# Layer 3's first chunk in a four-layer mixture-of-experts kernel: the inputs scaled ahead are made one layer-2 unit later

## The chip, the core and the metric

The kernel runs on one core of a Trainium2 chip. The core has TensorE (PE, with PEld for its weight loads), VectorE (DVE), ScalarE (ACT), GpSimd (POOL) and SyncE (SP), which here only issues DMAs. The metric is the device time of one execution in microseconds (us), lower is better.

## The reference

Four blocks follow each other on x of shape 8 x 128 x 128 (batch, time, width), each of the form x = x + ffn(cond(x)). Cut to what matters here:

```python
# layer 2: cond is a low-rank and a dense product with a gelu, ffn is
for e in range(8):                                   # 8 experts, H=128, F=512
    hdn = gelu(flat @ w1[e] + b1[e])
    out = out + (hdn @ w2[e] + b2[e]) * comb[:, e:e+1]
# layer 3: cond is a recurrence over time
next_h = tanh(xw_t + prev_h @ Wh)
# ffn is a mixture over 12 experts, weighted on the input side
h = sum_e (x @ W1[e].T) * dw1[:, e]                  # = sum_e (x * dw1[:, e]) @ W1[e].T
h = gelu(h)
y = sum_e (h @ W2[e].T) * dw2[:, e] + dw3 @ b2
```

Layer 3 adds over the experts before its gelu, so the kernel multiplies the input by each expert's weight first and lets TensorE accumulate all 12 products in one PSUM bank.

## The kernel before

Time is cut into four chunks of 32 steps, which is 256 columns (32 steps x 8 batch rows) or two tiles of 128. The work of layers 0 to 2 is written out as a list UNITS of 176 units, and every engine runs its own loop over the same slots n = 0 to 177. A unit of stream B is half an expert of layer 2: two 128-column pieces of the up product on PE into bank U (each in three passes, since operands are split into a high and a low part), then a gelu with bias on ACT into `gated`, and two slots later half of the down product on PE into bank Y. When both halves of an expert are there, DVE adds Y times the expert's weight into `acc_b` (two instructions, one for each tile). The last 16 units, 160 to 175, are layer 2 of the last chunk. They are called B0 to B15 here, and "slot B10" is n = 170.

In these slots three other jobs run beside layer 2:

- layer 3's recurrence of chunk 0: two steps in each slot up to B11. A step is a small product on PE into ZR and a tanh on ACT into `h`. Every PE step waits for the tanh of the step before.
- layer 3's down weights: each slot DVE turns one of 12 (`l_dn_turned`), ACT copies it to its high part (`l_dn_hi`), and DVE makes the low part (`l_dn_lo`) of the first six.
- layer 3's first scaled inputs, which are what the change moves. For each pair of experts j = 0 to 5, DVE multiplies the input by the weights that a DMA spread over all partitions (`l_weighted<-l_bc,l_in`, called w0 to w5 here), ACT copies the product to its high part (`scaled_hi`, s0 to s5), and the low part (`scaled_lo`, low 0 to low 5) is made by POOL for j in POOL_FIRST = [0, 1, 2, 4] and by DVE for j = 3 and 5. `l_weighted` has two buffers, so w_j waits until low j-2 is made.

The table AHEAD holds one slot number for each j. DVE scales in slot AHEAD[j] + 1, ACT copies in slot AHEAD[j] + 2, and DVE makes its low parts in slot AHEAD[j] + 3. POOL has no slots: it takes its low parts in order, as they come.

Within a slot the engines keep this order, and each waits in order. ACT: first step's `h`, the unit's two gelus, `scaled_hi`, `l_dn_hi`, second step's `h`. PE: the up product, the first step's ZR, the down product of the unit two slots back, the second step's ZR. DVE: `acc_b` of the unit three slots back if it closes an expert, the turning, `l_dn_lo`, the low part, the scaling. After the loop DVE adds the last expert (B14 and B15) to `acc_b`, PE turns the sum into bank M (`layer_sum`) and goes on with layer 3's up products; DVE adds the residual in `layer_sums`.

Of the kernel before, what the change touches and what calls it, by code (L numbers as in the profile page):

```python
# [13 lines left out]
CT = 32  # L14
# [4 lines left out]
E3 = 12  # L19
# [25 lines left out]
def layer_units(stream, k, first=0, last=LU):  # L45

    return [(stream, i, k) for i in range(first, last)]


UNITS = L0_UNITS[:-HOLD] + layer_units("A", 0) + L0_UNITS[-HOLD:]  # L50
# [7 lines left out]
C3 = AT["A", 0, CHUNKS - 1]  # L58
# [8 lines left out]
def unit(n):  # L67

    return UNITS[n] if 0 <= n < len(UNITS) else ("", 0, 0)
# [30 lines left out]
L3_ADDR, L3_SCORE, L3_DW, W2_SLOT = [C3 + CT // 2 + i for i in (0, 1, 9, 6)]  # L100
POOL_FIRST = [0, 1, 2, 4]
W2_LATE = 6
AHEAD = [C3 + CT - 4 + j for j in range(E3 // 2)]


def x_early(n):
# [44 lines left out]
def at(start, n):  # L151

    return slice(start, start + n)
# [19 lines left out]
def adaln_ffn_program(nc, a, out):  # L173
    with ExitStack() as ctx:
# [413 lines left out]
        def _(sc):  # L588
# [106 lines left out]
            def scaled_first_high(j):  # L695
                sc.wait_ge(weighted_full, j + 1)
                sc.wait_ge(u_full, AT["B", 2 * j + 1, CHUNKS - 1] + 1)
                nc.scalar.activation(scaled[0][:, 2 * j:2 * j + 2, :].rearrange("p e n -> p (e n)"), l3_weighted[:, j % 2, :],
                                     ACT.Copy).then_inc(scaled_hi, 1)

            def l3_high(n):
                if n - 1 in AHEAD:
                    scaled_first_high(AHEAD.index(n - 1))
                if n in W1_SLOTS:
                    e = W1_SLOTS.index(n)
                    sc.wait_ge(w1_turned, e + 1)
                    nc.scalar.activation(l3_up[0][:, e, :], l3_up_turned[:, e, :], ACT.Copy).then_inc(w1_hi, 1)
                if 0 <= n - 1 - W2_SLOT < E3:
                    e = n - 1 - W2_SLOT
                    sc.wait_ge(w2_turned, e + 1)  # L710
                    nc.scalar.activation(l3_dn[0][:, e, :, :], l3_dn_turned[:, e, :, :], ACT.Copy).then_inc(w2_hi, 1)
# [48 lines left out]

            for n in range(SLOTS, AHEAD[-1] + 3):
                if n - 2 in AHEAD:
                    scaled_first_high(AHEAD.index(n - 2))

            def idle(*_):
                pass
# [34 lines left out]
        def _(dve):  # L801
# [3 lines left out]
            def tt(out, in0, in1, op):  # L805
                return v.tensor_tensor(out=out, in0=in0, in1=in1, op=op)  # L806
# [231 lines left out]
            def taken(*name):  # L1038
                dve.wait_ge(m_full, m_of(*name) + 1)
                return bank_of(*name)  # L1040
# [89 lines left out]
            def layer_sums(n):  # L1130

                stream, i, k = unit(n - 3)
                if (stream, i) == ("A", LU - 1):
                    x = x1[:, at(k * N, N)]
                    tt(x, x, taken("sum0", k)[:, 0:N], ALU.add).then_inc(m_free, 1)
                    tt(z1m[:, :].rearrange("p (t b) -> p t b", b=B), taken("zp", k)[:, N:].rearrange("p (t b) -> p t b", b=B),
                       rank_mask[:, 0:B].unsqueeze(1).to_broadcast([P, CT, B]), ALU.mult).then_inc(z_scaled, 1)
                if (stream, i) == ("B", LU - 1):
                    tt(x3[:, at(k * N, N)], x1[:, at(k * N, N)], taken("sum1", k)[:, 0:N], ALU.add).then_inc(m_free, 1)
                stream, i, k = unit(n - 4)  # L1140
                if (stream, i) == ("A", LU - 1):
                    dve.wait_ge(l2_gelu, k + 1)
                    own(v.tensor_copy(l2_x[0][:, :], l2_in[:, :]))
                    tt(l2_x[1][:, :], l2_in[:, :], l2_x[0][:, :], ALU.subtract).then_inc(m_free, 1)
# [72 lines left out]
            def l3_scale_first(j):  # L1217

                if j == 0:
                    dve.wait_ge(dw_loaded, 16)  # L1220
                if j >= 2:
                    dve.wait_ge(*low_of(j - 2))
                tt(l3_weighted[:, j % 2, :].rearrange("p (e n) -> p e n", e=2), bc_of(j),
                   l3_in.unsqueeze(1).to_broadcast([P, 2, N]), ALU.mult).then_inc(weighted_full, 1)

            def l3_low_first(j):

                dve.wait_ge(scaled_hi, j + 1)
                dve.wait_ge(y_full, DOWNS.index(AT["B", 2 * j + 1, CHUNKS - 1]) + 1)
                tt(scaled[1][:, 2 * j:2 * j + 2, :].rearrange("p e n -> p (e n)"), l3_weighted[:, j % 2, :],  # L1230
                   scaled[0][:, 2 * j:2 * j + 2, :].rearrange("p e n -> p (e n)"), ALU.subtract).then_inc(scaled_odd, 1)
# [16 lines left out]
            def l3_ahead(n):  # L1248

                if n - 3 in AHEAD and AHEAD.index(n - 3) not in POOL_FIRST:  # L1250
                    l3_low_first(AHEAD.index(n - 3))
                if n - 1 in AHEAD:
                    l3_scale_first(AHEAD.index(n - 1))
# [62 lines left out]

            add_layer(len(UNITS) - 1)

            layer_sums(len(UNITS) + 2)
            for n in range(SLOTS, AHEAD[-1] + 4):  # L1320
                l3_ahead(n)

            def l3(c, route_next):
                m0, y0 = M0_L3 + c * M_L3, Y0_L3 + c * Y_L3
# [44 lines left out]
        def _(pe):  # L1369
# [262 lines left out]
            def idle(*_):  # L1632
                pass
# [148 lines left out]
```

## Time and profile before

| what | us |
|---|---|
| median of 3 runs | 625.62 (625.25 to 625.73) |
| the profiled execution, whole | 626.07 |
| its span from first to last instruction | 624.3 |
| PE busy in it | 601.4 (96%) |
| mean granted TensorE clock | 0.995 of full speed |

The profiled execution lies 0.45 us over the median, and 1.8 us of its time lie outside the span. Times in the rows below are us from the start of the span.

### The profile page before, as it was taken

Reading aid. Unit: us, or ns where it says so; the run is one execution under the profiler, and the core shown is the slowest. Engines: PE = TensorE matmul, PEld = TensorE weight load, DVE = VectorE, ACT = ScalarE, POOL = GpSimd, SP = SyncE. Lnnn points to the kernel's source line nnn. Section 1 sums busy time; section 2 is a strip of 40 time slices with the busy share of each in tenths; the row PEclk is TensorE's granted clock in tenths of the full one; section 3 lists DMA queues with packets and bytes.
Section 4 is the critical chain, followed back from the end, with each engine's and each line's share of the span. In section 5 each row is a group of like instructions: output and inputs, shape, how many; then the busy total and the mean of one; then the engine's idle time right before and its main releaser. Section 6 shows DMA issues by size and latency. Waiting matters only on the chain.

```text
span 624.3 us, 12421 instructions
## 1 busy us (share of the span) xinstructions
PE 601.4 (96%) x4526; PEld 562.4 (90%) x4526; DVE 348.0 (56%) x1221; ACT 287.5 (46%) x955; POOL 110.7 (18%) x328
## 2 busy tenths in 40 slices
PE   8889999999999999999999999999899999999896
PEld 8678788889999999999999999999889889898895
DVE  4865655765464455455553563158858665775414
ACT  3275645645655456455564556646723323311110
POOL 3134121111111111111111110000201221321410
PEclk9999999999999999999999999999999999999999
DMA  8998000000000000000000000090202102002000
GB/s 253 383 270 135 1 1 2 2 2 1 2 2 1 2 1 2 2 2 1 2 1 1 2 2 2 17 187 21 83 2 69 40 5 102 6 5 104 8 1 8
DMA packets 47477, 26.98 MB, mean 43 GB/s; under 512 B 28424, under 2 KB 42680, under 8 KB 46904
## 3 DMA queue, kind: packets, MB, share of 16 engines
q1 hardware_dynamic: 45392, 25.71, 15.2%
q8 instruction: 36, 0.59, 0.4%
q10 hardware_dynamic: 2024, 0.48, 0.4%
q14 instruction: 25, 0.20, 0.1%
HBM read 25.61 MB, written 0.57 MB: 42 GB/s over the span
## 4 chain that ended last, share of the span: by engine, by line
PE 80%; DVE 11%; ACT 3%; issue 2%; DMA 2%; POOL 1%; SPq 0%; DVEq 0%; POOLq 0%
PE Y L1371 32%; PE U L1371 29%; PE HH L1371 8%; PE ZR L1371 7%; PE M L1371 5%; DVE acc_a L814 2%; DMA l_bc<-dw 1%; DVE acc_b L814 1%; DVE rh L814 1%; DVE rank L846 1%; POOL scaled_lo L566 1%; DVE relu L806 1%; ACT gated L648 0%; DVE cmp_a L806 0%; DVE l_dn_turned L1092 0%
## 5 line engine op out<-in xcount | busy, mean ns | idle before, releaser
L1371 PE MATMUL Y<-l_dn,gated 128*128 128x128 f32 x1152 | 162.8, 284 | 1.8 <-ACT gated L648 0.8
L1371 PEld LDWEIGHTS Y<-l_dn,gated 128*128 128x128 f32 x1152 | 141.1, 192 | 3.5 <-issue 1.7
L648 ACT ACTIVATE gated<-U,b1T 128x256 f32<-128x256 f32 x256 | 106.7, 473 | 0.0
L1371 PE MATMUL U<-l_x_hi,l_up_hi 128*128 128x256 f32 x256 | 82.7, 323 | 0.0
L630 ACT ACTIVATE h<-ZR,rnn_b 128x8 f32<-128x8 f32 x128 | 34.2, 267 | 90.0 <-PE ZR L1371 87.6
L814 DVE SCALAR_TENSOR_TENSOR fresh<-zr_s,cand 128x8 f32<-128x8 f32 x128 | 21.4, 167 | 94.9 <-ACT cand L626 92.4
L1371 PE MATMUL U<-l_x_hi,l_up_lo 128*128 128x256 f32 x256 | 72.0, 281 | 0.0
L1371 PE MATMUL U<-l_x_lo,l_up_hi 128*128 128x256 f32 x256 | 71.9, 281 | 0.0
L550 POOL TENSOR_SCALAR zh<-zr_s 128x8 f32<-128x8 f32 x128 | 25.7, 200 | 253.4 <-ACT zr_s L622 253.4
L626 ACT ACTIVATE cand<-HH 128x8 f32<-128x8 f32 x128 | 22.7, 178 | 97.0 <-PE HH L1371 97.0
L1371 PE MATMUL U<-scaled_hi,l_up_hi 128*128 128x256 f32 x192 | 58.0, 302 | 1.7 <-POOL scaled_lo L566 1.7
L1371 PE MATMUL U<-scaled_hi,l_up_lo 128*128 128x256 f32 x192 | 54.3, 283 | 0.0
L1371 PE MATMUL U<-scaled_lo,l_up_hi 128*128 128x256 f32 x192 | 54.2, 282 | 0.0
L1371 PEld LDWEIGHTS HH<-rh,gru_u 128*128 128x128 f32 x256 | 39.3, 190 | 13.6 <-DVE rh L814 12.5
L1371 PEld LDWEIGHTS U<-l_x_hi,l_up_hi 128*128 128x128 f32 x256 | 48.7, 190 | 0.5 <-issue 0.4
L1371 PEld LDWEIGHTS U<-l_x_hi,l_up_lo 128*128 128x128 f32 x256 | 48.7, 190 | 0.0
L1371 PEld LDWEIGHTS U<-l_x_lo,l_up_hi 128*128 128x128 f32 x256 | 48.3, 189 | 0.0
L1371 PE MATMUL ZR<-h_gru,gru_u 128*128 128x8 f32 x256 | 47.3, 257 | 0.0
L1371 PEld LDWEIGHTS ZR<-h,rnn_w 128*128 128x128 f32 x256 | 41.0, 190 | 6.7 <-ACT h L630 4.4
L814 DVE SCALAR_TENSOR_TENSOR acc_a<-Y,mix,acc_a 128x128 f32<-128x128 f32 x96 | 33.7, 351 | 22.7 <-PE Y L1371 19.9
L1371 PE MATMUL HH<-rh,gru_u 128*128 128x8 f32 x256 | 40.5, 230 | 5.2 <-DVE rh L814 4.4
L1371 PEld LDWEIGHTS HH<-h_gru,gru_u 128*128 128x128 f32 x256 | 39.8, 192 | 4.4 <-DVE h_gru L814 3.1
(263 smaller groups left out, 1202.8 us busy)
## 6 DMA issues: line engine op xcount, KB each, us to landing
l_bc<-dw SPq DMA_DIRECT2D x4, 1536.0 KB, 6.7
stage<-L_ffn_W_dram SPq DMA_DIRECT2D x4, 768.0 KB, 10.4
w_raw<-L_ffn_W_dram SPq DMA_DIRECT2D x12, 256.0 KB, 7.0
l_up_raw<-L_ffn_W_dram SPq DMA_DIRECT2D x1, 2048.0 KB, 9.7
l_up_raw<-L_ffn_w_dram SPq DMA_DIRECT2D x1, 2048.0 KB, 14.6
l0f_up<-L_ffn_w_dram SPq DMA_DIRECT2D x1, 768.0 KB, 7.0
l0f_dn<-L_ffn_w_dram SPq DMA_DIRECT2D x1, 768.0 KB, 8.8
x<-x_dram SPq DMA_DIRECT2D x1, 512.0 KB, 4.2
```

The costliest lines, as they stand in the source:

```text
L550: own(nc.gpsimd.tensor_scalar(zh[:, :], zr_s[:, 0, :], -0.5, 0.5, ALU.mult, ALU.add))
L566: nc.gpsimd.tensor_tensor(out=scaled[1][:, 2 * j:2 * j + 2, :].rearrange("p e n -> p (e n)"), in0=source[:, j % 2, :], in1=scaled[0][:, 2 ...
L626: nc.scalar.activation(cand[:, :], HH[:, at(N + step % CT * B, B)], ACT.Tanh).then_inc(gru_cand, 1)
L630: nc.scalar.activation(h3[:, at((step + 1) * B, B)], ZR[:, at(step % CT * B, B)], ACT.Tanh, bias=rnn_b[:, 0:1]).then_inc(rnn_h, 1)
L648: last = nc.scalar.activation(gated[:, n % 4, h * N:(h + 1) * N], U[n % 2][:, h * N:(h + 1) * N], ACT.Gelu, bias=b1T[:, col:col + 1])
L806: return v.tensor_tensor(out=out, in0=in0, in1=in1, op=op)
L814: return v.scalar_tensor_tensor(out=out, in0=in0, scalar=scalar, in1=in1, op0=op0, op1=op1)
L846: own(v.tensor_reduce(out=grp(rank, g, n), in_=ca, axis=AX.X, op=ALU.add))
L1371: return nc.tensor.matmul(out, lhsT, rhs, start=start, stop=stop, skip_group_check=shared)
```

## The change

The table AHEAD starts one slot later, so that w_j, s_j and DVE's low parts stand one slot on. Two pieces of DVE's code after the loop change places; the `for` loop there runs from 178 to AHEAD[-1] + 4, which is 177 before and 178 now, so that it has no turns in either kernel and the exchange moves nothing.

```diff
-AHEAD = [C3 + CT - 4 + j for j in range(E3 // 2)]
+AHEAD = [C3 + CT - 3 + j for j in range(E3 // 2)]
...
             add_layer(len(UNITS) - 1)
 
-            layer_sums(len(UNITS) + 2)
             for n in range(SLOTS, AHEAD[-1] + 4):
                 l3_ahead(n)
+            layer_sums(len(UNITS) + 2)
```

AHEAD was 168 to 173 and is 169 to 174. PE, POOL and SP have the same rows in the same order in both kernels.

ScalarE around slot B10, before. The first pair of gelus is unit B10's, the second B11's, and `l_dn_hi` is a copy of a down weight.

```order
L648 ACTIVATE gated<-U,b1T 128x256 x2
L698 ACTIVATE scaled_hi<-l_weighted 128x512
L711 ACTIVATE l_dn_hi<-l_dn_turned 128x512
L630 ACTIVATE h<-ZR,rnn_b 128x8 x2
L648 ACTIVATE gated<-U,b1T 128x256 x2
```

The same place on ScalarE now.

```order
L648 ACTIVATE gated<-U,b1T 128x256 x2
L711 ACTIVATE l_dn_hi<-l_dn_turned 128x512
L630 ACTIVATE h<-ZR,rnn_b 128x8 x2
L648 ACTIVATE gated<-U,b1T 128x256 x2
L698 ACTIVATE scaled_hi<-l_weighted 128x512
```

The copy s0 no longer stands between B10's gelus and the two recurrence steps, but behind B11's gelus. Each later copy moves in the same way, and s5 stands alone in slot B16, behind the last gelus.

VectorE in slots B9 and B10, before. The `acc_b` pair is the expert of units B6 and B7.

```order
L1092 STREAM_TRANSPOSE l_dn_turned<-w_raw 128x4x4x32
L806 TENSOR_TENSOR l_dn_lo<-l_dn_turned,l_dn_hi 128x512
L806 TENSOR_TENSOR l_weighted<-l_bc,l_in 128x512
L814 SCALAR_TENSOR_TENSOR acc_b<-Y,comb_l,acc_b 128x128 x2
L1092 STREAM_TRANSPOSE l_dn_turned<-w_raw 128x4x4x32
L806 TENSOR_TENSOR l_dn_lo<-l_dn_turned,l_dn_hi 128x512
```

The same place on VectorE now.

```order
L1092 STREAM_TRANSPOSE l_dn_turned<-w_raw 128x4x4x32
L806 TENSOR_TENSOR l_dn_lo<-l_dn_turned,l_dn_hi 128x512
L814 SCALAR_TENSOR_TENSOR acc_b<-Y,comb_l,acc_b 128x128 x2
L1092 STREAM_TRANSPOSE l_dn_turned<-w_raw 128x4x4x32
L806 TENSOR_TENSOR l_dn_lo<-l_dn_turned,l_dn_hi 128x512
L806 TENSOR_TENSOR l_weighted<-l_bc,l_in 128x512
```

The first scaling w0 stands behind one sum, one turning and one low part of a weight that it stood ahead of.

VectorE from slot B13 to the end of layer 2, before. The scalings are w4 and w5, the low parts 3 and 5, and the sums those of B10/B11, B12/B13 and B14/B15.

```order
L806 TENSOR_TENSOR l_weighted<-l_bc,l_in 128x512
L814 SCALAR_TENSOR_TENSOR acc_b<-Y,comb_l,acc_b 128x128 x2
L806 TENSOR_TENSOR scaled_lo<-l_weighted,scaled_hi 128x512
L806 TENSOR_TENSOR l_weighted<-l_bc,l_in 128x512
L814 SCALAR_TENSOR_TENSOR acc_b<-Y,comb_l,acc_b 128x128 x2
L806 TENSOR_TENSOR scaled_lo<-l_weighted,scaled_hi 128x512
L814 SCALAR_TENSOR_TENSOR acc_b<-Y,comb_l,acc_b 128x128 x2
L806 TENSOR_TENSOR x<-x,M 128x256
```

The same place on VectorE now.

```order
L814 SCALAR_TENSOR_TENSOR acc_b<-Y,comb_l,acc_b 128x128 x2
L806 TENSOR_TENSOR l_weighted<-l_bc,l_in 128x512
L806 TENSOR_TENSOR scaled_lo<-l_weighted,scaled_hi 128x512
L806 TENSOR_TENSOR l_weighted<-l_bc,l_in 128x512
L814 SCALAR_TENSOR_TENSOR acc_b<-Y,comb_l,acc_b 128x128 x2
L806 TENSOR_TENSOR scaled_lo<-l_weighted,scaled_hi 128x512
L814 SCALAR_TENSOR_TENSOR acc_b<-Y,comb_l,acc_b 128x128 x2
L806 TENSOR_TENSOR x<-x,M 128x256
```

Only w4 has changed places, with the sum of B10/B11; w5 and the low parts 3 and 5 keep theirs among VectorE's rows, and low 5 stood ahead of the last sum before as well.

## Rows read from the trace of the kernel before

**Rows 1.** The page: busy time of each engine over the span.

```profile
PE 601.4 (96%) x4526; PEld 562.4 (90%) x4526; DVE 348.0 (56%) x1221; ACT 287.5 (46%) x955; POOL 110.7 (18%) x328
```

**Rows 2.** Waits from 436 to 458: who waited, for whom, total, times, longest.

```profile
ACT scaled_hi L698 <- DVE l_weighted L806: 2.3, 3, 1.2
...
PE ZR L1371 <- ACT h L630: 1.7, 1, 1.7
```

**Rows 3.** The chain that ended last, from 435: start, duration, what.

```profile
435.30 7.62 DMA l_bc<-dw
```

**Rows 4.** TensorE's timeline: start, duration, line, operation, [idle before, releaser].

```profile
441.05 0.39 PE L1371 MATMUL ZR<-h,rnn_w 128*128 128x8 f32 x2
...
445.03 0.39 PE L1371 MATMUL ZR<-h,rnn_w 128*128 128x8 f32 x2 [1.66 <-ACT h L630]
...
454.23 2.05 PE L1371 MATMUL Y<-l_dn,gated 128*128 128x128 f32 x16 [0.78 <-ACT gated L648]
...
456.98 0.71 PE L1371 MATMUL M<-ident,acc_b 128*128 128x128 f32 x4 [0.27 <-DVE acc_b L814]
...
457.77 0.47 PE L1371 MATMUL U<-scaled_hi,l_up_hi 128*128 128x256 f32 x1
```

**Rows 5.** ScalarE's timeline, slots B9 to B15.

```profile
439.32 0.27 ACT L630 ACTIVATE h<-ZR,rnn_b 128x8 f32<-128x8 f32 x1 [0.48 <-PE ZR L1371]
...
441.47 0.27 ACT L630 ACTIVATE h<-ZR,rnn_b 128x8 f32<-128x8 f32 x1 [0.48 <-PE ZR L1371]
441.64 0.83 ACT L648 ACTIVATE gated<-U,b1T 128x256 f32<-128x256 f32 x2
443.67 0.63 ACT L698 ACTIVATE scaled_hi<-l_weighted 128x512 fp32r<-128x512 f32 x1 [1.20 <-DVE l_weighted L806]
444.21 0.61 ACT L711 ACTIVATE l_dn_hi<-l_dn_turned 128x512 fp32r<-128x512 f32 x1
...
445.62 0.83 ACT L648 ACTIVATE gated<-U,b1T 128x256 f32<-128x256 f32 x2
...
448.04 0.83 ACT L648 ACTIVATE gated<-U,b1T 128x256 f32<-128x256 f32 x2
448.75 0.64 ACT L698 ACTIVATE scaled_hi<-l_weighted 128x512 fp32r<-128x512 f32 x1
...
453.30 0.87 ACT L648 ACTIVATE gated<-U,b1T 128x256 f32<-128x256 f32 x2
```

**Rows 6.** VectorE's timeline, slots B9 to the last sum.

```profile
441.21 0.65 DVE L806 TENSOR_TENSOR l_dn_lo<-l_dn_turned,l_dn_hi 128x512 fp32r<-128x512 f32 x1
442.94 0.69 DVE L806 TENSOR_TENSOR l_weighted<-l_bc,l_in 128x512 f32<-128x512 f32 x1 [1.09 <-DMA l_bc<-dw]
443.55 0.60 DVE L814 SCALAR_TENSOR_TENSOR acc_b<-Y,comb_l,acc_b 128x128 f32<-128x128 f32 x2
444.19 0.71 DVE L1092 STREAM_TRANSPOSE l_dn_turned<-w_raw 128x512 f32<-128x512 f32 x1
444.82 1.37 DVE L806 TENSOR_TENSOR l_dn_lo<-l_dn_turned,l_dn_hi 128x512 fp32r<-128x512 f32 x1
...
447.35 0.64 DVE L806 TENSOR_TENSOR l_weighted<-l_bc,l_in 128x512 f32<-128x512 f32 x1
...
453.02 1.79 DVE L806 TENSOR_TENSOR l_weighted<-l_bc,l_in 128x512 f32<-128x512 f32 x1
...
455.57 0.69 DVE L806 TENSOR_TENSOR scaled_lo<-l_weighted,scaled_hi 128x512 fp32r<-128x512 f32 x1 [0.23 <-DVE acc_b L814]
456.31 0.61 DVE L814 SCALAR_TENSOR_TENSOR acc_b<-Y,comb_l,acc_b 128x128 f32<-128x128 f32 x2
```

**Rows 7.** GpSimd's timeline, its low parts 0, 1 and 4.

```profile
444.38 1.27 POOL L566 TENSOR_TENSOR scaled_lo<-l_weighted,scaled_hi 128x512 fp32r<-128x512 f32 x1 [74.11 <-ACT scaled_hi L698]
447.54 1.61 POOL L566 TENSOR_TENSOR scaled_lo<-l_weighted,scaled_hi 128x512 fp32r<-128x512 f32 x1 [1.89 <-ACT scaled_hi L698]
...
453.00 1.27 POOL L566 TENSOR_TENSOR scaled_lo<-l_weighted,scaled_hi 128x512 fp32r<-128x512 f32 x1 [1.99 <-ACT scaled_hi L698]
```

## The prediction, made blind

> **What bounds the kernel now.** I read the page first: TensorE is busy for 601.4 of 624.3 us [rows 1], so whatever does not reach TensorE's order of work is worth nothing, and the time to be won in a stretch is what TensorE idles there. Next come the waits of the stretch from 436 to 458, which holds every instruction that the change moves. Three entries matter. ScalarE waited three times, 2.3 us together, for `l_weighted`, and TensorE waited once, 1.7 us, for ScalarE's `h` [rows 2]. The timelines tie them together. The transfer of the spread weights `l_bc` takes 7.62 us and lands at 442.92 [rows 3], VectorE's first scaling w0 waits 1.09 us for it and starts at 442.94 [rows 6], and ScalarE's copy s0 stands idle 1.20 us for w0 and starts at 443.67 [rows 5]. Behind s0 in ScalarE's order are the copy of a down weight and the recurrence's tanh of slot B10. TensorE's next recurrence product needs that tanh, so it starts at 445.03 after 1.66 us of nothing [rows 4]. This is a stall of the whole chain, not of a side job.
>
> A second limit follows it. From B12 to B15 ScalarE has two gelus, a scaled copy and a weight copy in each slot and no idle time: its gelus start at 448.04 and 453.30 three slots apart, 1.753 us a slot [rows 5]. TensorE's last two down products wait for the last gelus and start at 454.23 [rows 4], their sums on VectorE start at 456.31 [rows 6], and the closing product with the sum starts 0.67 us behind that, at 456.98 [rows 4]. So I ask for two things: when the gelus of B15 now start, and whether VectorE is free when the last Y is full.
>
> **ScalarE and TensorE from slot B10.** With s0 gone from slot B10, ScalarE goes from the gelus to the weight copy and the tanh, as in the slots before it, where one `h` follows the same one of the last slot by 2.15 us (439.32 and 441.47) [rows 5]. TensorE's product stands 2.15 after 441.05, at 443.20, not at 445.03 [rows 4]: 1.83 us earlier. ScalarE's `h` of B11 is at 443.62, its gelus at 443.79, and s0 is wanted 0.71 later (448.04 to 448.75), at 444.50 [rows 5].
>
> Is w0 there by then? VectorE ends its low part of slot B9 at 441.86 and now goes straight into the sum of B6/B7, at about 441.78, since neighbours overlap by some 0.08. The steps of the rows are 0.64 for a sum, 0.63 for a turning and about 0.57 for a low part that nothing disturbs (the 0.65 of its own less that overlap) [rows 6]: turning at 442.42, low part at 443.05, w0 from 443.62 to 444.30. The transfer landed 0.70 before that, and s0 has 0.2 to spare. So the transfer's wait is covered by 1.8 us of work that VectorE had to do anyway.
>
> From s0 on ScalarE steps by 0.54 to the weight copy [rows 5], by 0.52 to the tanh and by 0.15 to the gelus of B12 (estimates, the first from the 0.54 and the 0.63 durations, the second from the 0.17 of 441.47 to 441.64): 445.71, where it was 448.04. Three slots of 1.753 lead to 450.97 for the gelus of B15: 2.33 us earlier. The 0.50 beyond 1.83 is the copy that slot B11 had to wait for (the second of the three waits). TensorE keeps up: before, too, it was TensorE that waited 0.78 for the last gelus [rows 4], so I cost nothing for it. Its last down products start at 451.90 and, 2.05 long, fill Y by 453.95.
>
> **VectorE and GpSimd in the same slots.** Here a stall can come back. The rows show that a VectorE operation of the form TENSOR_TENSOR and a GpSimd one do not run together. The low part at 444.82 took 1.37 where its twin took 0.65, and ended 0.54 after GpSimd's (444.38 + 1.27 = 445.65) [rows 6, 7]. In the other direction GpSimd's low 1 took 1.61 when it started at 447.54 in w2 (447.35 to 447.99): 1.27 from w2's end, less than 0.1 of it unexplained [rows 6, 7]. And w5 began at 453.02, 0.02 after low 4, and took 1.79 [rows 6, 7]. The first to start keeps the other out. Sums and turnings show no such loss (0.60 and 0.71 throughout).
>
> With that I go through VectorE's new order. Sum of B8/B9 and the turnings lie between the scalings. w1 at 444.85 to 445.50, ahead of low 0 (s0 ends 445.13, GpSimd follows 0.08 later, as 444.38 follows the 444.30 at which s0 ended before [rows 5, 7]), which then runs to 446.77. w2 waits for low 0 and runs 446.81 to 447.47; low 1 ends 448.74. w3 waits for low 1 and starts at 448.78, while low 2 may start when s2 is made, at 448.89: VectorE is first by 0.11. w3 ends 449.46 and low 2 450.73; the sum of B10/B11 fits between; w4 450.77 to 451.46; low 3 451.38 to 452.07; w5 452.11 to 452.80, ahead of low 4, which could start at 452.42 (s4 at 451.70): first by 0.31. Low 4 then holds GpSimd's side until 454.07. The sum of B12/B13 is not held. s5 is ScalarE's, from 452.84 to 453.47, so that low 5 could begin at 453.51, and it is kept out until 454.07 and ends 0.54 later, at 454.61.
>
> **The closing sum.** Low 5 stands ahead of the last `acc_b` on VectorE. Before, it ran at 455.57 to 456.26, just in front of the sum at 456.31, and cost nothing since Y was not full yet [rows 6]. Now Y is full at 453.95 and the sum could start at 453.99, but low 5 lets it start only at 454.53, a new wait of 0.54. Queued behind it are that sum, TensorE's closing product, and all of layer 3. The product starts 0.67 later, at 455.20.
>
> **Sum.** 456.98 - 455.20 = 1.78 us: 1.83 for the recurrence's stall, plus 0.50 on ScalarE, less 0.54 for low 5 in front of the sum (0.01 is rounding). Layer 3's first products follow from the same product, before 0.79 behind it (457.77) [rows 4]. They want the pair j = 5 only at the eleventh of twelve experts, and low 4 and low 5 are both made before the first, so nothing is late there. From there to the end the order and the data are those of before, and what waits, waits on TensorE. No DMA is issued by another time but those that follow the chain. I take the gain through to the end unchanged.
>
> The profiled execution took 626.07, so it would take 624.29. The median of the runs is 0.45 lower, 625.62, and I predict 625.62 - 1.78 = **623.8 us**.
>
> One rule of the Trainium skill speaks against this change: SBUF — State Buffer, section "Who interferes with whom", says that a VectorE instruction with two SBUF inputs and a GpSimd instruction that reads SBUF take the same read port, and that the second to issue waits for all of the first. By it low 5 pays and the sum is 1.78; the 1.37 and 1.79 of this trace agree with it. Were there no such exclusion, the same walk gives low 5 from 453.41 to 454.10, the closing product at 454.69, and a gain of 2.29.
>
> **Rivals.**
>
> *The low part is not in the way: 2.3 us, 623.3.* This holds if w5 and s5 come early enough, or the two engines overlap better than at 444.82, so that the closing sum starts when Y is full. For it speaks that low 5 needs to be only 0.54 earlier. Against it are the rows with 1.37 and 1.79. Chance 0.12.
>
> *GpSimd wins a race.* If it starts low 2 ahead of w3 (my margin is 0.11), w3 ends near 450.63, s3 and with it the gelus of B15 slip by 0.75, and low 5 ends near 455.0: the closing product at 455.60, a gain of 1.4, 624.2. If it is low 4 ahead of w5 (margin 0.31, and this is what happened before, by 0.02), low 5 ends near 455.6 and the gain is 0.8, 624.9. Chance 0.13 and 0.07.
>
> *No change: the wait only moves.* If w0 came late for s0 in slot B11, the tanh of the second step is late there as well. But B11 has the last recurrence step of the chunk, and no product waits for it until layer 3. Also both races lost together: low 4 and low 5 then end near 455.7 and 456.4, the closing product at 456.95, gain 0.03. Time 625.0 to 625.6. Chance 0.09.
>
> *Slower.* The mechanism is again low 5 ahead of the last sum, now later than it was: low 4 starts first, w5 waits for it, s5 for w5, low 5 for s5, four links of which each now comes a slot nearer to the end. It turns the gain into a loss when low 5 ends after 456.39 (0.08 overlap before 456.31), which is 1.78 after my 454.61; at 457.7 it would cost 1.3, time 626.9. That needs one more GpSimd instruction (1.27) in front of it than I can find, on top of both races. Chance 0.05.
>
> **How the numbers follow.** My forecast (gain 1.55 to 2.05) has 0.54; the five cases above 0.12, 0.13, 0.07, 0.09 and 0.05. The bounds are the walk without exclusion (2.3) and the late low 5 (0.8); 0.1 to 0.2 on each side covers that the medians of three runs scatter by 0.25. Range 623.1 to 624.9, which leaves 0.09, 0.05 and part of the 0.07 out. A measurement of this kernel tells about 0.2%, 1.25 us, from no change. Faster by that: 0.54 + 0.12 and most of the 0.13, 0.77. Within: 0.18. Slower: 0.05.
>
> **What would show it.** Right: no idle time of TensorE before a recurrence product near 443.2; ScalarE's s0 without a wait worth 0.1; gelus of B15 near 451.0; a VectorE low 5 of over 1 us or a late start of the closing sum behind it; the closing product near 455.2. Wrong: a wait of s0 or s3 for `l_weighted`, a w3 or w5 of over 1.2 us, or a span after the closing product that isn't the old 167.3 us (624.3 - 456.98). I would be wrong above all if a scaling and a GpSimd low part swapped places in that closest race.

## The result, and the profile after

Over 20 runs of each kernel the ratio of the changed kernel to the one before is 0.9964, 95% interval 0.995 to 0.9979. The medians are 624.34 us for the changed kernel and 626.30 us for the one before. Applied to the 625.62 us that the prediction started from, the ratio is 623.4 us, a gain of 2.25 us (1.3 to 3.1). Predicted were 623.8, a gain of 1.78, and a range of 623.1 to 624.9.

The profiled execution after took 624.21 us with a span of 622.5, where the one before took 626.07 with 624.3. That difference of 1.86 us is not the change alone. ScalarE's gelus of B8, before anything that the change moves, start at 436.12 and started at 437.33, so 1.21 us came from the early part of the execution. From those gelus to the closing product is 17.52 us and was 19.65 (437.33 to 456.98 [rows 4]): 2.13 us, the change's own. And from the closing product to the end of the span are 168.9 us, where they were 167.3: 1.5 us were lost again, for a reason given below. So all readings below use the distance from the gelus of B8. In the kernel before they are this row of ScalarE's timeline, two pairs of gelus ahead of B10's at 441.64 [rows 5]:

```profile
437.33 0.83 ACT L648 ACTIVATE gated<-U,b1T 128x256 f32<-128x256 f32 x2
```

One profiled execution in the experiments, that of the kernel with AHEAD one slot less than before, was a disturbed one with a span of 646.6 us, and only its waits are relied on, not its two distances in the table.

The timeline of ScalarE in the changed kernel, from the gelus of B8 on; `scaled_hi` is the copy of a scaled input.

```profile
436.12 0.83 ACT L648 ACTIVATE gated<-U,b1T 128x256 f32<-128x256 f32 x2
...
440.43 0.83 ACT L648 ACTIVATE gated<-U,b1T 128x256 f32<-128x256 f32 x2
...
442.58 0.83 ACT L648 ACTIVATE gated<-U,b1T 128x256 f32<-128x256 f32 x2
443.30 0.64 ACT L698 ACTIVATE scaled_hi<-l_weighted 128x512 fp32r<-128x512 f32 x1
...
444.49 0.85 ACT L648 ACTIVATE gated<-U,b1T 128x256 f32<-128x256 f32 x2
...
449.76 0.89 ACT L648 ACTIVATE gated<-U,b1T 128x256 f32<-128x256 f32 x2
```

Slot B10 (440.43) to slot B11 (442.58) is again the ordinary 2.15 us, where it was 3.98 [rows 5], and no row carries a wait for `l_weighted`. B11 to B12 is 1.91, where it was 2.42.

TensorE in the changed kernel: the product that stalled before [rows 4], the last down products, and the closing product.

```profile
441.99 0.39 PE L1371 MATMUL ZR<-h,rnn_w 128*128 128x8 f32 x2
...
450.70 2.05 PE L1371 MATMUL Y<-l_dn,gated 128*128 128x128 f32 x16 [0.68 <-ACT gated L648]
...
453.64 0.71 PE L1371 MATMUL M<-ident,acc_b 128*128 128x128 f32 x4 [0.46 <-DVE acc_b L814]
```

The 1.66 us of waiting for ScalarE's `h` are gone. The last down products start 14.58 us after B8's gelus (16.90 before), 2.32 earlier; the closing product 2.13 earlier.

VectorE in the changed kernel, w0 to w5 with the last two low parts and sums.

```profile
442.40 0.68 DVE L806 TENSOR_TENSOR l_weighted<-l_bc,l_in 128x512 f32<-128x512 f32 x1
...
443.62 0.65 DVE L806 TENSOR_TENSOR l_weighted<-l_bc,l_in 128x512 f32<-128x512 f32 x1
...
445.46 0.68 DVE L806 TENSOR_TENSOR l_weighted<-l_bc,l_in 128x512 f32<-128x512 f32 x1
...
447.32 0.69 DVE L806 TENSOR_TENSOR l_weighted<-l_bc,l_in 128x512 f32<-128x512 f32 x1 [0.56 <-POOL scaled_lo L566]
...
449.27 0.69 DVE L806 TENSOR_TENSOR l_weighted<-l_bc,l_in 128x512 f32<-128x512 f32 x1 [0.74 <-POOL scaled_lo L566]
449.88 0.68 DVE L806 TENSOR_TENSOR scaled_lo<-l_weighted,scaled_hi 128x512 fp32r<-128x512 f32 x1
450.60 0.69 DVE L806 TENSOR_TENSOR l_weighted<-l_bc,l_in 128x512 f32<-128x512 f32 x1
...
452.29 0.78 DVE L806 TENSOR_TENSOR scaled_lo<-l_weighted,scaled_hi 128x512 fp32r<-128x512 f32 x1 [0.48 <-DVE acc_b L814]
452.99 0.59 DVE L814 SCALAR_TENSOR_TENSOR acc_b<-Y,comb_l,acc_b 128x128 f32<-128x128 f32 x2
```

GpSimd in the changed kernel: its four low parts.

```profile
444.01 1.40 POOL L566 TENSOR_TENSOR scaled_lo<-l_weighted,scaled_hi 128x512 fp32r<-128x512 f32 x1 [74.97 <-ACT scaled_hi L698]
445.94 1.35 POOL L566 TENSOR_TENSOR scaled_lo<-l_weighted,scaled_hi 128x512 fp32r<-128x512 f32 x1 [0.52 <-ACT scaled_hi L698]
447.70 1.46 POOL L566 TENSOR_TENSOR scaled_lo<-l_weighted,scaled_hi 128x512 fp32r<-128x512 f32 x1 [0.42 <-ACT scaled_hi L698]
451.24 1.28 POOL L566 TENSOR_TENSOR scaled_lo<-l_weighted,scaled_hi 128x512 fp32r<-128x512 f32 x1 [2.07 <-ACT scaled_hi L698]
```

Low 5 at 452.29 takes 0.78 where its twin at 449.88 took 0.68, since low 4 runs until 452.52. Y is full at 452.75 (450.70 + 2.05), and the last sum starts at 452.99 behind low 5, 0.24 later. In the kernel before it started 0.03 after Y was full (456.28 to 456.31 [rows 4, 6]), so low 5 costs 0.21 here.

Why the end of this execution was longer, by stretches: the length of the stretch, the busy times of PE, PEld, DVE, ACT and POOL with their numbers of instructions, then PEclk, the granted clock as a share of full speed, and two figures for the DMA engines. First the changed kernel around the start of chunk 3.

```profile
582.00:590.00 8.00, 6.27 (x38) 5.86 (x37) 0.35 (x2) 0.93 (x2) 2.50 (x2) 0.79 0.04 8
```

The same place in the kernel before.

```profile
584.00:592.00 8.00, 6.28 (x51) 5.87 (x50) 1.64 (x4) 1.23 (x2) 2.80 (x3) 1.00 0.04 10
```

Both kernels idle there for 1.47 and 0.26 us (TensorE waits for a low part of chunk 3), but in the execution after, the clock fell behind it. 8 us at a mean of 0.79 are 1.7 us of work lost (8 x 0.21), about the size of what is missing. The change doesn't touch this place, and in another profiled execution of the changed kernel it stands at 1.00:

```profile
587.00:595.00 8.00, 6.28 (x50) 5.96 (x50) 0.21 (x2) 0.78 (x2) 2.50 (x2) 1.00 0.04 8
```

Of the twelve profiled executions in this document five have the clock fall at this place: this one, and those of the kernels "only the copies later" (its first), "only the scalings later", "low 5 behind the sum" and "low 5 on GpSimd" below. So it comes with and without the change, and from the closing product to the end these five take 168.8 to 169.3 us. The others take 167.3 to 167.4, but for one whose clock falls elsewhere, which is told below.

### The profile page after: what moved, and what is told of

It reads as the page before. It is cut to its first block, busy times and chain, and to the rows that moved or that the text cites. A ratio compares the mean times of both kernels' runs of the same rounds, so it can differ in the third digit from the quotient of the medians.

```text
span 622.5 us, 12422 instructions
## 1 busy us (share of the span) xinstructions
PE 601.4 (97%) x4526; PEld 562.2 (90%) x4526; DVE 345.9 (56%) x1221; ACT 287.3 (46%) x955; POOL 111.0 (18%) x328
## 4 chain that ended last, share of the span: by engine, by line
PE 83%; DVE 10%; ACT 3%; issue 2%; POOL 0%; DVEq 0%; POOLq 0%
PE Y L1371 33%; PE U L1371 30%; PE HH L1371 8%; PE ZR L1371 7%; PE M L1371 5%; DVE acc_a L814 2%; ACT gated L648 1%; DVE acc_b L814 1%; DVE rh L814 1%; DVE rank L846 1%; DVE cmp_a L806 0%; DVE fresh L814 0%; ACT cand L626 0%; POOL scaled_lo L566 0%; DVE cmp_b L806 0%
```

## The experiments

The table has every kernel's own distances from one profiled execution each, from the gelus of B8, and its ratio to the kernel before. "Stall" is TensorE's wait before a recurrence product in slots B9 to B11.

| kernel | stall | last down products | closing product | ratio (95% interval) |
|---|---|---|---|---|
| before | 1.66 | 16.90 | 19.65 | |
| changed | none | 14.58 | 17.52 | 0.9964 (0.995 to 0.9979) |
| changed, again | none | 14.57 | 17.52 | 0.996 (0.9941 to 0.998) |
| only the copies later | none | 14.56 | 17.91 | 1.0024 (1.0008 to 1.004) |
| the same, again | none | 15.50 | 19.78 | one run, 629.47 us |
| only the scalings later | 2.34 | 18.32 | 21.08 | 1.004 (1.0026 to 1.0054) |
| one slot less than before | 3.84 | 21.05 | 23.87 | 1.0037 (1.0015 to 1.0058) |
| first pair's transfer ahead | 0.50 | 15.71 | 18.47 | 0.9971 (0.9953 to 0.999) |
| one slot more than changed | none | 14.42 | 18.94 | 1.001 (0.9989 to 1.0031) |
| changed, low 5 behind the sum | none | 14.56 | 17.39 | 0.9979 (0.996 to 0.9998) |
| changed, low 5 on GpSimd | none | 14.58 | 17.41 | 0.9942 (0.9918 to 0.9965) |
| low 5 behind, weight copies late | none | 13.9 | 16.76 | 0.9945 (0.9923 to 0.9966) |

In ten of these executions the first transfer of the spread weights landed 7.5 to 7.7 us after its issue. The exceptions are the first one with only the copies later, with 6.1, and the one whose transfer was cut in two.

**Which half of the change carries the gain?** First only ScalarE's copies.

```diff
+AHEAD_ACT = [n + 1 for n in AHEAD]
...
-                if n - 1 in AHEAD:
-                    scaled_first_high(AHEAD.index(n - 1))
+                if n - 1 in AHEAD_ACT:
+                    scaled_first_high(AHEAD_ACT.index(n - 1))
```

> ScalarE's six copies stand one slot later, VectorE stays as in the kernel before. My measure is the time from the gelus of B8 to the closing product with acc_b: 19.65 us before (437.33 to 456.98), 17.52 us in the changed kernel (436.12 to 453.64). Theory (the copy s0 ahead of the recurrence's tanh is the cause): TensorE's 1.7 us stall is gone and the last two down products start about 14.6 us after B8's gelus, as in the changed kernel (16.9 before). But VectorE's w5 then meets GpSimd's low 4 and low 5 is late, so that the closing product may come only 18.2 to 19.3 us after B8. Rival (VectorE's new order is the cause): stall and all distances as before, 16.9 and 19.65.

The stall is gone and the last down products come at 14.56, as expected; the closing product at 17.91, a little before the expected 18.2 to 19.3. But the runs put it 0.24% behind the kernel before, 1.5 us. In the profiled execution the transfer had landed after 6.1 us and w0 had no wait, and eleven of the twelve runs scatter from 624.4 to 629.3 us, so the same kernel was profiled again.

> A second look at the kernel in which only ScalarE's copies stand later. Its 12 runs scatter from 624.4 to 629.3 us, and in the first look the transfer had landed in 6.1 us. Theory (w0 still stands ahead of a sum and a low part on VectorE, so a landing after 7.7 us delays all of VectorE's row): with the usual landing w0 waits over 1 us, w1 meets low 0 and takes over 1.2 us, s1 waits, and the closing product comes 19.3 to 20.5 us after B8, against 17.91 in the first look. Rival (the scatter has nothing to do with the transfer): 17.9 again.

VectorE in the second execution: w0, the last weight work behind it, w1, and w5 further on.

```profile
446.14 0.69 DVE L807 TENSOR_TENSOR l_weighted<-l_bc,l_in 128x512 f32<-128x512 f32 x1 [1.15 <-DMA l_bc<-dw]
...
448.02 0.65 DVE L807 TENSOR_TENSOR l_dn_lo<-l_dn_turned,l_dn_hi 128x512 fp32r<-128x512 f32 x1
448.59 1.77 DVE L807 TENSOR_TENSOR l_weighted<-l_bc,l_in 128x512 f32<-128x512 f32 x1
...
456.59 1.65 DVE L807 TENSOR_TENSOR l_weighted<-l_bc,l_in 128x512 f32<-128x512 f32 x1
```

With a landing after 7.7 us w0 waits 1.15, w1 meets low 0 and takes 1.77, and s1 waits for it. Later w5 starts inside low 4 (456.42) and takes 1.65, with two sums and low 5 queued behind it, and the closing product comes at 19.78, inside the expected 19.3 to 20.5. In the first execution w5 started 0.14 ahead of low 4 (451.31 and 451.45) and took 0.69. With the usual landing, then, moving the copies takes the stall from TensorE and gives it all back at the closing sum. VectorE's order is no bystander: the scaling had to move too, so that a sum, a turning and the low part of a weight fill the time of the transfer. The 19.78 explain "no gain", not the 1.5 us by which the runs are worse.

Then only VectorE's part, with ScalarE as before.

```diff
+AHEAD_DVE = [n + 1 for n in AHEAD]
...
-                if n - 3 in AHEAD and AHEAD.index(n - 3) not in POOL_FIRST:
-                    l3_low_first(AHEAD.index(n - 3))
-                if n - 1 in AHEAD:
-                    l3_scale_first(AHEAD.index(n - 1))
+                if n - 3 in AHEAD_DVE and AHEAD_DVE.index(n - 3) not in POOL_FIRST:
+                    l3_low_first(AHEAD_DVE.index(n - 3))
+                if n - 1 in AHEAD_DVE:
+                    l3_scale_first(AHEAD_DVE.index(n - 1))
```

> VectorE's scalings and low parts stand one slot later, ScalarE's copies stay. Theory: s0 still stands ahead of the tanh and now waits for a w0 that ends near 444.3 and not 443.6, so TensorE's stall before a recurrence product grows from 1.7 to about 2.3 us; the wait of s1 goes in exchange. Closing product 19.6 to 20.1 us after B8's gelus, time as before or up to 0.5 us more. Rival (VectorE's new order is the cause): 17.5 us, and 2 us less in all.

The stall is 2.34, as the theory said, but the closing product comes at 21.08 and not 19.6 to 20.1. What is missing goes with TensorE's clock. Its product behind the stall, and the stretches of 2 us around it:

```profile
444.47 0.39 PE L1372 MATMUL ZR<-h,rnn_w 128*128 128x8 f32 x2 [2.34 <-ACT h L631]
```

```profile
442.00:444.00 2.00, 0.13 (x2) 0.00 (x0) 2.00 (x4) 0.89 (x2) 0.18 (x1) 1.00 0.00 0
444.00:446.00 2.00, 1.53 (x12) 1.54 (x12) 0.27 (x1) 1.52 (x6) 1.40 (x1) 0.86 0.00 0
446.00:448.00 2.00, 2.00 (x11) 2.00 (x11) 1.83 (x4) 1.24 (x4) 1.28 (x1) 0.50 0.02 4
448.00:450.00 2.00, 2.00 (x16) 2.00 (x15) 1.51 (x3) 1.72 (x4) 0.72 (x1) 0.79 0.00 0
450.00:452.00 2.00, 2.00 (x20) 2.00 (x20) 1.06 (x3) 1.99 (x5) 0.65 (x1) 1.00 0.00 0
```

Behind an idle time of 2.34 us the granted clock went from 1.00 to 0.50, from 2.4 to 1.2 GHz, and was back by 450; 11 products ran in the 2 us from 446, where the stretch from 450, at full clock, has 20. The lost work is 1.7 us in these rows (2 x 0.14 + 2 x 0.50 + 2 x 0.21), part of it in the shadow of ScalarE. The runs put this kernel 2.5 us behind the kernel before (1.6 to 3.4), the distance 1.43. By the runs neither half of the change gains anything by itself.

**Is it the transfer?** Two experiments on the kernel before. AHEAD one slot earlier (`C3 + CT - 5`):

> AHEAD one slot earlier than in the kernel before (167 to 172). Distances are from the gelus of B8: 19.65 us to the closing product before. Theory (the copy s0 waits for the transfer, with the recurrence behind it): s0 now stands in slot B9 and still can't start before the transfer has landed, so TensorE's stall grows from 1.7 us by nearly one slot of 2.15, to 3.5 to 3.9 us, and the closing product comes 21 to 22 us after B8; 1.3 to 2.3 us slower in all. Where the transfer lands 1.5 us early, as it did in the one look at the kernel with the late copies only (6.1 and not 7.7 us), the loss is smaller by as much. Rival (the position of s0 in a slot costs a fixed time, whatever the transfer does): 19.6 us, no change.

ScalarE waits 3.39 us for w0, TensorE 3.84:

```profile
461.82 0.63 ACT L698 ACTIVATE scaled_hi<-l_weighted 128x512 fp32r<-128x512 f32 x1 [3.39 <-DVE l_weighted L806]
```

```profile
463.18 0.60 PE L1371 MATMUL ZR<-h,rnn_w 128*128 128x8 f32 x2 [3.84 <-ACT h L630]
```

The stall is one slot (2.15) plus the old 1.66, as it must be when s0 has to wait for the same landing from one slot earlier. In this execution the clock was 1.00 up to the stall and fell behind it (mean 0.83 from 462 to 482), and the closing product comes at 23.87, beyond the expected 21 to 22. Over the runs the kernel is 0.37% slower, 2.3 us (0.9 to 3.6). The 2.18 us by which the stall grew would make that up alone, so whether the clock falls behind it in the other executions too stays open.

Then the order of before, with the transfer cut in two. VectorE's w0 waits for the first part alone, w1 for the second.

```diff
-                sp.dma_start(l3_bc[:, :, :].rearrange("p e n -> p (e n)"),
-                             dw1[c, :, :].rearrange("e n -> (e n)").unsqueeze(0).to_broadcast([P, N * E3])).then_inc(dw_loaded, 16)
+                for e0, ne in ((0, 2), (2, E3 - 2)) if c == 0 else ((0, E3),):
+                    sp.dma_start(l3_bc[:, at(e0, ne), :].rearrange("p e n -> p (e n)"),
+                                 dw1[c, at(e0, ne), :].rearrange("e n -> (e n)").unsqueeze(0).to_broadcast([P, N * ne])
+                                 ).then_inc(dw_loaded if ne > 2 else dw_first, 16)
```

> The kernel before with its order, and the transfer of the spread weights cut in two: the first pair's 256 KB by itself, then the other 1280 KB. w0 waits for the first only. Theory (transfer, then w0, then s0, then tanh): w0 starts when VectorE is free, 1.1 us earlier, the wait of s0 falls from 1.2 us to under 0.3, TensorE's stall from 1.7 to under 0.8, closing product 17.9 to 18.6 us after B8's gelus (19.65 before). Rival (the order itself is the cause, not the transfer): 19.6 us.

ScalarE and TensorE with the cut transfer:

```profile
441.09 0.83 ACT L651 ACTIVATE gated<-U,b1T 128x256 f32<-128x256 f32 x2
441.95 0.63 ACT L701 ACTIVATE scaled_hi<-l_weighted 128x512 fp32r<-128x512 f32 x1
```

```profile
443.31 0.39 PE L1374 MATMUL ZR<-h,rnn_w 128*128 128x8 f32 x2 [0.50 <-ACT h L633]
```

The first 256 KB land after 4.4 us, s0 starts 0.86 behind the gelus and not 2.03, the stall is 0.50, and the closing product 18.47, all inside what the theory gave. With no instruction moved, 1.18 of the 2.13 us come back. So the late transfer is the cause of 1.16 of the 1.66 us of stall. The other 0.50 is left with the transfer out of the way: s0's own place ahead of the tanh, with its step of 0.54, is the part that only the order removes.

**What does low 5 in front of the last sum cost?** Two kernels on top of the changed one. Low 5 behind `add_layer`:

```diff
             add_layer(len(UNITS) - 1)
 
-            for n in range(SLOTS, AHEAD[-1] + 4):
-                l3_ahead(n)
+            l3_low_first(5)
             layer_sums(len(UNITS) + 2)
```

> The changed kernel with VectorE's low part 5 behind the last acc_b. Theory: the last sum starts when Y is full, 0.2 us earlier; closing product 17.3 us after B8's gelus (17.52 in the changed kernel), layer 3 doesn't wait for low 5; total 0.2 us less, which the runs can't tell apart. Rival (something else holds the sum): 17.5 still.

And low 5 on GpSimd (`POOL_FIRST = [0, 1, 2, 4, 5]`):

> The changed kernel with low part 5 made by GpSimd behind low 4. Theory (low 5 ahead of the last sum on VectorE costs 0.2 us): the last sum starts when Y is full, as with low 5 behind the sum, closing product 17.3 to 17.4 us after B8 (17.52 changed, 17.39 with low 5 behind the sum). GpSimd ends low 5 about 2.7 us after w5, before layer 3 wants it, so no new TensorE wait. Rival (GpSimd is now late for layer 3's eleventh expert): a wait of TensorE for scaled_lo about 3.6 us after layer 3's first product.

The closing product comes at 17.39 and 17.41, 0.13 and 0.11 before the changed kernel's; I had expected 0.2. In the first of them the sum waits for Y and no longer for low 5:

```profile
452.81 0.61 DVE L814 SCALAR_TENSOR_TENSOR acc_b<-Y,comb_l,acc_b 128x128 f32<-128x128 f32 x2 [1.02 <-PE Y L1370]
453.46 0.69 DVE L806 TENSOR_TENSOR scaled_lo<-l_weighted,scaled_hi 128x512 fp32r<-128x512 f32 x1
```

The last sum starts 0.11 after Y is full in both (here 450.65 + 2.05 = 452.70), and not 0.03 as in the kernel before, so that only 0.13 of the 0.24 come back. Layer 3 waited for neither. The ratios can't tell these two from the changed kernel.

**One slot more** (`C3 + CT - 2`), with which the loop behind the slots has a turn and puts low 5 behind the last sum.

> AHEAD one more slot later (170 to 175). s0 then has no recurrence tanh behind it at all, and low 5 stands behind the last sum through the loop that now has a turn. Theory: the stall was gone already, so only 0.1 to 0.3 us come on top: closing product 17.2 to 17.4 us after B8, and no wait in layer 3 since low 5 is wanted 3.6 us after its first product. Rival (each slot later brings another 2 us, or the late low parts now hold layer 3): 15.5 us, or a TensorE wait for scaled_lo after the closing product.

The last down products come 0.16 earlier, but the closing product 1.42 later than in the changed kernel, at 18.94 where I had expected 17.2 to 17.4, and the runs show no gain over the kernel before. I had missed VectorE's chain:

```profile
451.43 0.69 DVE L806 TENSOR_TENSOR l_weighted<-l_bc,l_in 128x512 f32<-128x512 f32 x1 [1.16 <-POOL scaled_lo L566]
...
452.68 0.69 DVE L806 TENSOR_TENSOR scaled_lo<-l_weighted,scaled_hi 128x512 fp32r<-128x512 f32 x1
453.40 1.64 DVE L806 TENSOR_TENSOR l_weighted<-l_bc,l_in 128x512 f32<-128x512 f32 x1
454.96 0.60 DVE L814 SCALAR_TENSOR_TENSOR acc_b<-Y,comb_l,acc_b 128x128 f32<-128x128 f32 x2
```

```profile
455.61 0.71 PE L1371 MATMUL M<-ident,acc_b 128*128 128x128 f32 x4 [2.04 <-DVE acc_b L814]
```

w4 waits for low 2, w5 then starts inside low 4 and takes 1.64, and the last sum stands behind w5: TensorE waits 2.04 us. This is the mechanism of my rivals "GpSimd wins a race" and "slower", one slot further on. The distance is still 0.71 better than before, but the granted clock fell behind this wait too, and in this execution 168.9 us follow the closing product instead of 167.3:

```profile
458.00:460.00 2.00, 2.00 (x11) 2.00 (x11) 0.00 (x0) 0.27 (x1) 0.00 (x0) 0.50 0.00 0
```

A gain of 0.71 less a loss of 1.6 fits a ratio of 1.001 (0.9989 to 1.0031).

**The next limit.** On the kernel with low 5 behind the sum, ScalarE's copies of down weights 8 to 11 leave slots B12 to B15.

```diff
+W2_HI_LATE = 8
...
-                if 0 <= n - 1 - W2_SLOT < E3:
+                if 0 <= n - 1 - W2_SLOT < W2_HI_LATE:
...
+            for e in range(W2_HI_LATE, E3):
+                sc.wait_ge(w2_turned, e + 1)
+                nc.scalar.activation(l3_dn[0][:, e, :, :], l3_dn_turned[:, e, :, :], ACT.Copy).then_inc(w2_hi, 1)
```

> The changed kernel with low part 5 behind the last sum, and with ScalarE's last four copies of down weights (8 to 11, which only layer 3's down products want) taken out of slots B12 to B15 and made behind s5. Theory (after the stall is gone ScalarE bounds B12 to B15 with 1.75 us a slot, of which such a copy is 0.52): the slots fall to TensorE's 1.6 us, gelus of B15 0.5 to 0.7 us earlier, last down products 14.0 us after B8's gelus (14.58), closing product 16.6 to 16.9 us (17.52 changed, 17.39 with only low 5 moved), 0.6 to 0.9 us less than the changed kernel in all. Rival (VectorE's chain of scalings and low parts bounds these slots by now): last down products or closing product no more than 0.2 us earlier.

> The changed kernel as it is, on the same chip, for a second look and a direct comparison. Theory: 17.5 us from B8's gelus to the closing product, whatever the early part of the run does, ratio to the kernel before 0.9955 to 0.9975. Rival (the local distance differs from run to run as much as the total): outside 17.4 to 17.6.

The closing product comes at 16.76, as expected, 0.76 before the changed kernel's. ScalarE now waits for TensorE:

```profile
449.64 0.84 ACT L649 ACTIVATE gated<-U,b1T 128x256 f32<-128x256 f32 x2 [0.25 <-PE U L1371]
...
451.24 0.84 ACT L649 ACTIVATE gated<-U,b1T 128x256 f32<-128x256 f32 x2 [0.25 <-PE U L1371]
```

The step is 1.60, TensorE's own. The last 16 down products run in one row with the 8 before them, so their 13.9 in the table is worked out (451.04 + 3.15 - 2.05, less 438.20). On one chip this kernel has a ratio of 0.9945 and the changed one 0.996; the intervals overlap, and by the runs alone the two aren't told apart. Its closing product is the earliest of all. The second profiled execution of the changed kernel gives 17.52 to the hundredth, though its execution took 627.57 us at a mean clock of 0.989.

## Why the prediction was right, point by point

**The stall and its cause** were right: product ZR without a wait, one slot of 2.15, 1.83 us back. The transfer's share of the stall is shown from both sides, by a transfer that lands earlier (0.50 left) and by an s0 that asks for it a slot earlier (3.84).

**The transfer's wait is covered** held: w0 starts 6.28 us after B8's gelus, with no wait; predicted 6.29 (443.62 less 437.33). That the cover is needed, and not only the copy's new place, is what the kernel with the copies only showed.

**ScalarE up to the gelus of B15**: predicted 13.64 us after B8's, measured 13.64 (449.76 less 436.12). Down products predicted at 14.57, measured 14.58.

**The closing sum** was mis-sized. I took the wait behind low 5 to be 0.54, and it is 0.21. The step that failed is "which then runs to 446.77" and its two repetitions: I let a GpSimd low part last 1.27 us from the end of the VectorE scaling that keeps it out. It ends 1.14 to 1.15 after that end in all three cases (444.27 to 445.41, 446.14 to 447.29, 448.01 to 449.16), as if 0.12 of its own time lay inside the wait. The rows had it [rows 6, 7]: from w2's end at 447.99 to low 1's end at 449.15 is 1.16, which I read as "1.27 from w2's end, less than 0.1 of it unexplained". Three times 0.12 made w5 0.3 us earlier than I had it, low 4 was not pushed by w5, and low 5 started where predicted (16.17 after B8's gelus, predicted 16.18) and met only 0.23 us of low 4. The local gain is 1.83 + 0.49 on ScalarE, less 0.19 for the later start of the closing product behind the last down products (2.94 after them, 2.75 before): 2.13. It lies just outside the 1.55 to 2.05 of my forecast, between it and my first rival. The runs (2.25, from 1.3 to 3.1) can't tell the three apart, so that the total came within 0.4 of the forecast says little about this term.

Had the wait been nothing, the gain would have been 2.3, my first rival; the two kernels that move low 5 show 2.26 and 2.24.

**The races** were not as close as I made them: w3 started 0.38 before low 2 (447.32 and 447.70), where I had 0.11, and w5 0.64 before low 4, where I had 0.31. The overlap that I left out worked for the change here: it made w3 and w5 ready earlier. The rivals with a lost race did not come, but the mechanism is real, as one slot more shows.

**From the closing product to the end** I took the old 167.3 us. It was 168.9 in the profiled execution, by a clock that fell behind an idle time that both kernels have, and 167.3 in the second execution of the changed kernel. Total times carry this; the distance inside the slots doesn't.

What stays open: the kernel with only the copies moved is 1.5 us slower than the kernel before by the runs, of which its second profiled execution explains 0.13. That execution's span is 3.4 us longer than the one of before, but 3.15 of it lie ahead of the gelus of B8, where the kernels have the same order. The runs of this kernel have lower mean clocks (six of the eleven at 0.987 to 0.992, where 26 of the 33 of before beside them are at 0.994 to 0.997). That its three TensorE waits close together (0.46, 0.88 and 1.83 us) let the clock fall in some executions would fit, but neither execution shows it: behind the 1.83 it stayed at 1.00.

## What to carry to other kernels

An engine that works in order passes a wait on to whatever stands behind it. Here a copy that TensorE did not need for another 13 us held a recurrence step, so the first question about side work is not what it costs but what is queued behind it when its input is late. Moving it helps only if the producer moves along, behind work that has to be done anyway; by the runs each half alone lost time. And there is an end to "later": one slot more turned the wait for the transfer into a wait of the closing sum for the same chain. Where total times scatter by more than the effect, compare the distance between two fixed instructions around the change: in the changed kernel it repeated to 0.01 us while the totals differed by 3. But it carries whatever varies between the two instructions. In the kernel with only the copies later it was 17.91 and 19.78, by a transfer that landed after 6.1 and 7.7 us, and the 19.65 of the kernel before rests on one execution, with the usual landing.

## What the runs showed of the hardware that I had not expected

TensorE's granted clock fell behind some stalls and not behind others. Idle times of 1.66 us (kernel before) and 1.83 us (only the copies later, the second execution) left it at 1.00. Behind 2.04 us (one slot more) and 2.34 us (only the scalings later) it went to 0.50 for a while. The 1.47 + 0.26 us at chunk 3 took it down in five executions of twelve, in one of the changed kernel and not in another. What decides that, no run here shows.

The Trainium skill, SBUF — State Buffer, section "Who interferes with whom", has the second of a VectorE instruction with two SBUF inputs and a GpSimd instruction that reads SBUF wait for the whole of the first. The traces agree on who waits, but the loser hides a part of its own time: GpSimd's low part ends 1.15 us after the scaling that kept it out and lasts 1.27 alone, and VectorE's low part of a weight ended 0.54 after GpSimd's [rows 6, 7] and lasts 0.65 alone. Over a chain of three such hand-overs this was the 0.35 us by which the local gain was mis-sized.
